# A GNN kernel: one wait, one load and two subtractions in other places of their queues

## The reference

```python
edge_index = jnp.stack([src, dst])
x = _layernorm(x + _L0_gnn_ref(x, src, dst, ...))       # attention, 12 heads of 64 channels
x = _layernorm(x + _L1_gnn_ref(x, edge_index, ...))     # 4 heads of 256, then 1 head of 768
```

```python
e = leaky_relu(a1[src] + a2[dst])
w = exp(e - segment_max(e, dst)[dst])
agg = segment_sum(w[:, :, None] * ft[src], dst) / segment_sum(w, dst)
```

## Time and profile before

| what | value |
|---|---|
| median of 3 runs | 1193.08 us (1192.1 to 1193.24) |
| profiled execution | 1192.1 us |
| its span, first to last instruction | 1190.3 us |
| PE busy | 1085.8 us, 91% |
| DVE busy | 993.9 us, 84% |
| ACT busy | 654.5 us, 55% |
| POOL busy | 145.4 us, 12% |
| mean granted clock of PE | 0.976 |

### The profile page before, as it was taken

One profiled execution on the slowest core, in us unless ns is written; L12 is line 12 of the kernel. 1 busy time (PEld: TensorE's weight loads), 2 busy tenths in 40 slices (PEclk: granted clock), 3 DMA queues, 4 the chain that ended last, 5 costly groups with the idle time before them and its releaser, 6 DMA issues.

```text
span 1190.3 us, 20787 instructions
## 1 busy us (share of the span) xinstructions
PE 1085.8 (91%) x7873; PEld 910.2 (76%) x7873; DVE 993.9 (84%) x1698; ACT 654.5 (55%) x1070; POOL 145.4 (12%) x155
## 2 busy tenths in 40 slices
PE   6887679988898898799999999999989999999996
PEld 3443556666666666699999899999978888788885
DVE  6988999999999999894884799999797765277864
ACT  6444989999899999422200377676712311232431
POOL 1000000000000000000036021020500025321111
PEclk9999879999999999999999999999989999999998
DMA  3011302020202110653045510204052024245111
GB/s 140 27 62 47 130 2 87 1 88 1 87 5 84 38 55 7 219 176 126 28 142 195 208 43 2 80 1 142 2 177 67 28 78 168 78 147 177 67 64 50
DMA packets 39858, 98.94 MB, mean 83 GB/s; under 512 B 4467, under 2 KB 17147, under 8 KB 39765
## 3 DMA queue, kind: packets, MB, share of 16 engines
q1 hardware_dynamic: 39766, 97.66, 24.1%
HBM read 70.74 MB, written 26.90 MB: 82 GB/s over the span
## 4 chain that ended last, share of the span: by engine, by line
PE 59%; DVE 25%; issue 10%; ACT 3%; DVEq 1%; DMA 1%; POOL 0%; SPq 0%; POOLq 0%; ACTq 0%
PE psum L1005 13%; PE psum L922 13%; PE psum L970 12%; DVE R L1539 12%; PE psum L1033 9%; DVE R L1525 6%; PE psum L701 3%; PE psum L955 3%; PE psum L986 1%; ACT R L1154 1%; PE psum L805 1%; PE psum L1016 1%; ACT R L1170 1%; DVE LC L1503 1%; DVE R L1401 1%
## 5 line engine op out<-in xcount | busy, mean ns | idle before, releaser
L864 PE MATMUL psum<-ident,R 128*128 128x128 f32 (+3 forms) x1200 | 161.0, 284 | 45.1 <-ACT R L1154 44.9
L864 PEld LDWEIGHTS psum<-ident,R 128*128 128x128 f32 (+3 forms) x1200 | 130.7, 144 | 86.8 <-ACT R L1154 74.2
L1539 DVE CUSTOM_DVE_ANT_0 R<-R,LC 128x1250 f32<-128x1250 f32 x120 | 176.0, 1468 | 0.0
L1154 ACT ACTIVATE R<-R,row_max 128x1250 f32<-128x1250 f32 x120 | 161.4, 1345 | 5.2 <-DVE row_max L1539 4.0
L878 PE MATMUL psum<-R 128*64 128x256 f32 (+3 forms) x1200 | 149.5, 388 | 0.0
L1170 ACT COPY R<-psum 128x1280 f32<-128x1280 f32 x120 | 143.3, 1194 | 1.5 <-PE psum L864 1.5
L922 PE MATMUL psum<-w_hi,x1T_hi 128*128 128x256 f32 (+1 forms) x480 | 136.3, 284 | 2.7 <-issue 1.6
L922 PE MATMUL psum<-w_lo,x1T_hi 128*128 128x256 f32 (+1 forms) x480 | 135.0, 281 | 0.0
L922 PE MATMUL psum<-w_hi,x1T_lo 128*128 128x256 f32 (+1 forms) x480 | 134.9, 281 | 0.0
L1525 DVE SCALAR_TENSOR_TENSOR R<-R 128x1250 f32<-128x1250 f32 x80 | 122.5, 1532 | 0.0
L1986 POOL TENSOR_TENSOR rstd<-rstd,minus_half 128x1 f32<-128x1 f32 (+1 forms) x40 | 30.5, 763 | 712.2 <-DVE rstd L1552 712.2
(11 more groups left out here) (223 smaller groups left out, 2569.8 us busy)
## 6 DMA issues: line engine op xcount, KB each, us to landing
R<-rows_spill SPq DMA_DIRECT2D x20, 625.0 KB, 5.2
rowbuf<-rows_spill SPq DMA_DIRECT2D x14, 625.0 KB, 5.3
lc_spill<-LC SPq DMA_DIRECT2D x9, 625.0 KB
LC<-lc_spill SPq DMA_DIRECT2D x9, 625.0 KB, 5.8
res_spill<-colbuf SPq DMA_DIRECT2D x36, 128.0 KB, 2.4
R<-res_spill SPq DMA_DIRECT2D x9, 512.0 KB, 3.4
R<-in_x_dram SPq DMA_DIRECT2D x1, 3456.0 KB
res_spill<-R SPq DMA_DIRECT2D x9, 384.0 KB
```

Source lines behind the costliest of these rows:

```text
L864: last = e.transpose(turn0[r % 2][0:m, s, 0:n_dst], ring[0:n_dst, r % RING0, s * P:s * P + m], ident[0:n_dst, 0:n_dst])
L1154: e.activation(ring[0:m, r % RING0, :], ring[0:m, r % RING0, :], ACT.Exp, bias=row_max[0:m, r % RING:r % RING + 1], scale=-1.0, accum_out= ...
L1539: e.tensor_tensor_reduce(slot, slot, LC[0:m, i, :], 1.0, MIN_CEILING, ALU.add, ALU.min, row_max[0:m, r % RING:r % RING + 1]).then_inc(S.le ...
```

## The change

It moves things and takes none out but one wait. In `dve_program` DVE waits for `cleared` to be 3, not 2, ahead of the count, and the waits inside the first addition go. In `sync_program` `load_w1(0)` and its wait go ahead of `store_x1(0)`. In the part that makes x1, `rest_w1(1)` goes ahead of `first_sum(1)`, and `rest_w1(0)` ahead of `first_norm(1)`. In `turn_after1` tile 1 is transposed (on PE, and kept on ACT) after product (2, 0) and no longer after (1, 0).

```diff
-        turn_after1 = {(2, i): i + 1 for i in range(1, NT - 2)}
-        turn_after1[(1, 0)] = 1
+        turn_after1 = {(2, i): i + 1 for i in range(NT - 2)}
         turn_after1[(0, NT - 2)] = NT - 1
...
             load_x0(4)
+            e.wait_ge(S.turned0, ROWS0 - 1)
+            load_w1(0)
             for i in range(NT):
...
                 store_x1(i)
                 if i == 0:
-                    e.wait_ge(S.turned0, ROWS0 - 1)
-                    load_w1(0)
                     for t in range(5, 9):
                         load_x0(t)
...
-            def add(g, half, first=False):
-                if first:
-                    e.wait_ge(S.cleared, 3)
+            def add(g, half):
                 e.wait_ge(S.win_free, g * GT + GT)
...
-                        add(g + (-1), 1 - half, first)
+                        add(g + (-1), 1 - half)
...
-            group(1, 1, True)
+            group(1, 1)
...
-                if g == 0:
-                    e.wait_ge(S.cleared, 3)
...
-            e.wait_ge(S.cleared, 2)
+            e.wait_ge(S.cleared, 3)
             span = e.value_load(base_i[0:1, GROUPS:GROUPS + 1], min_val=0, max_val=N)
...
             rest_x1(0)
+            rest_w1(1)
             for i in range(1, NT):
                 first_sum(i)
-                if i == 1:
-                    rest_w1(1)
                 if 1 < i < 4:
                     rest_x1(i - 1)
                 first_stats(i)
+                if i == 1:
+                    rest_w1(0)
                 if i >= 4:
                     rest_x1(i - 1)
                 first_norm(i)
-                if i == 1:
-                    rest_w1(0)
```

More of the change, by code:

```diff
@@ L1411, in add, with group @@
                 e.tensor_tensor(window_, window_, window_psum(half), ALU.add).then_inc(S.win_added, 1)
-            def group(g, half, first=False):
+            def group(g, half):
                 for j in range(GT):
```

## The result

The change makes the kernel slower. Its median is 1199.1 us (1197.73 to 1202.31, six runs), beside 1193.62 us (1192.1 to 1194.94, six runs) of the kernel before; the ratio over all executions on record, 25 of the kernel after, is 1.0054 with an interval of 1.0039 to 1.0068, that is 6.4 us, 4.7 to 8.1 (the two medians alone lie 5.5 apart). The forecast was slower by 4.4, with a range that ended at 6.2. The profiled execution of the kernel after took 1199.95 us with a span of 1198.1, 7.8 us more than the span before.

What follows compares the result with a forecast made beforehand. DVE was taken to set the pace in the edge count and up to 516.07, before gemm1. Start 2.6 plus second place 1.8 made +4.4 us, 1197.5 by the median, range 1194.6 to 1199.3.

Steps and rivals of the forecast that it cites:

- Step 1: Start of the edge count: DVE's wait for the third clear delays everything behind it, +2.6 us, bounds 1.6 to 3.0.
- Step 2: Before gemm1: w1 block 0's load goes out earlier, gemm1 starts near 489.5 not 492.37; gain on PE, not the chain.
- Step 3: Store of x1 tile 0, behind 768 KB of load, lands +1.3 us later, bounds 0 to 3.0; DVE waits for it.
- Step 4: DVE, rest_w1(1) ahead of first_sum(1): same 1.67 us instruction 3.3 us earlier, input ready; nothing either way.
- Step 5: DVE, rest_w1(0) ahead of first_norm(1): fills GpSimd wait, later work 0.7 us earlier; x1 tile 1 ready later, 497.1 with store.
- Step 6: Tile 1's transposes before the second product: PE waits till 497.1, clock drops; 516.07 moves +1.8, bounds -0.7 to +3.6.
- A: Rival, chance 0.22: start's delay passes, second place even or better; +1.9 to +3.2 us, about 1195.6.
- B: Rival, chance 0.10: start's delay is absorbed before 124 us; +1.8 or less, 1194.9.
- C: Rival, chance 0.05: PE's earlier first product sets the end, second place -2.9; -0.3 in sum, down to 1190.2.
- D: Rival, chance 0.03: nothing measurable, both places under 0.5 us; needs the clearing complete when DVE asks.

Runs made afterwards that it cites:

- e1: Kernel before with one edit: DVE waits for the third clear ahead of the count; ratio 1.0028 to before, +3.3 us.
- e3: Kernel before with load_w1(0) issued ahead of store_x1(0) and nothing else; ratio 1.0033 to before, +3.9 us.
- e10: Kernel before with the load of w1 block 0 issued from ACT's queue, ahead of the store on SP's queue; ratio 1.0011 to before, +1.3 us.
- e11: Kernel before with the load of w1 block 0 halved, 384 KB ahead of the store and 384 behind; ratio 1.0012 to before, +1.4 us.
- e12: Kernel before with load_w1(0) ahead of store_x1(0) and first_sum(1) ahead of rest_x1(0) on DVE; 1193.03 us, ratio 0.9987 to before.
- e4: Kernel before with the new orders of rest_w1 and of tile 1's transposes, load and store as before; ratio 1.0012 to before, +1.4 us.
- e7: Kernel after with the start of before and rest_w1(0) behind first_norm(1) again; ratio 1.0019 to the kernel before, +2.3 us.

## Why the prediction was right in sign and too low

- **Step 1, the start, +2.6**: right in mechanism. 15.03 for 15.0, and e1 alone costs 3.3 (1.5 to 5.2). The size rests on one profile whose first one-hot was the earliest of twelve; against their mean the delay is 2.1. The first leaky0 came at 128.31, not 127.0: 1.26 us that came with PE's lower clock after the count, which no step has.
- **Step 2, the load, issued at 480.5, landed about 486, gemm1 at 489.5**: the issue was right and the landing wrong. It took 7.6 us where I reckoned 5.5, since I moved 768 KB at 375 GB/s and the stretch had 235 to 296, shared with the store and the x0 loads; for the 0.9 us to the landing, too, the prediction shows no row. ACT kept 1.34 us of idle time and PE gained 1.4, not 2.9. As step 2 says, this gain isn't on the chain; e3 shows that, with PE's first product earlier and a longer time.
- **Step 3, "+1.3 us. Bounds: 0 ..., 3.0"**: this is the term that was mis-sized. The mechanism, a store held up by the bytes of a load ahead of it, is shown (e3, e10, e11, e12), and even the 1.1 us between the two landings was about right (0.96). But the store took 6.10 us for 3.18, +2.9, at my upper bound, since the load ahead of it lands 2.1 us later than I took. I had the row for it, the 6.8 us of the earlier trace rows, and used it for the bound only. The rule in step 3's aside, the order within a ring, isn't needed: from the other queue the load costs 2.5 of the 3.0 us.
- **Step 4, nothing**: not contradicted; no run moves rest_w1(1) alone.
- **Step 5, the subtraction fills 0.66 us of idle time, -0.7**: failed. It took the power and the subtraction to run side by side. GpSimd's power takes 2.0 us beside this subtraction, so the norm waits 0.45 us after it. From the table of the stretch: the norm and the subtraction were done 24.11 us after the last leaky0 before, 23.98 in e4. The gain is 0.1.
- **Step 6, PE waits for tile 1 and its clock falls**: right. The idle time was 6.17 us ("4 us or more"), the clock fell to 0.50, and from the transposes to the product it took 525.80 - 505.17 = 20.63 us, for which I had 19.3 + 1.4 = 20.7. Only the hand-over was late: 499.4 net for 497.1, of which 1.6 is step 3's and 0.5 step 5's; 0.2 I haven't traced. That PE's lateness would outweigh DVE's rests on the traces; no run leaves out the new place of the transposes alone.
- **The sum**: 2.65 + 3.98 = 6.6 us by the two places, +6.4 measured. I had 2.6 + 1.8. The 2.2 missing are steps 3 (1.6) and 5 (0.5). That 6.6 meets 6.4 so closely is in part luck: with the mean start it is 6.1, and the single times of e7 and e10 lie 1.7 to 1.8 us under what their traces say. The rest of the profile's 7.8, +3.10 ahead of the last leaky0 and -1.9 at the end, are differences between single executions, which cancel in part.

Of the rivals, A fell with the 6.10 us of the store and B with e1; C fell as argued, the first product being earlier in e3 and the kernel slower; D fell with the first one-hot and the stretch. That PE sets the end and not DVE holds for the kernel after, by 0.8 us (DVE's low part of tile 3 is there at 525.0, the product starts at 525.80); e7 shows that the margin is thin.

Three things stay open: why the store of tile 2 lands after 3.9 to 4.3 us in e4, e7 and e12 and after 2.3 before, since no run isolates what it meets; whether the low clock at 117 to 126 us is likelier with the late start (it is there in both profiles with the late start, and in 4 of the 12 without it, with a fifth in part); and the times of e7 and e10, above.

## What to carry to other kernels

A load issued earlier isn't free because its target buffer is: ask which transfer in flight somebody waits for, and add all the bytes in flight with it, at the rate of that stretch and not the best one. Before an engine's order is changed to fill an idle gap, look for what runs on the neighbour in that gap, and whether the trace has the same pair side by side elsewhere. A wait that can't be shortened is best covered: first_sum(1) in front of it brought back 2.6 of the 3.0 us of the stretch that moving the load had cost. And a term read from one profile, like the start's 2.6, is to be read in a second one first.

## What the runs showed of the hardware

GpSimd's power of 128x1 elements takes 0.55 us while DVE waits for it, and 2.00 beside a DVE subtraction of 1.75 us with both inputs in SBUF; it then ends 0.41 us after the subtraction does. GpSimd's timeline after, first the stretch of x1, then layer 2:

```profile
487.40 0.55 POOL L1980 TENSOR_TENSOR rstd<-rstd,minus_half 128x1 f32<-128x1 f32 x1 [482.15 <-DVE rstd L1547]
502.40 2.00 POOL L1980 TENSOR_TENSOR rstd<-rstd,minus_half 128x1 f32<-128x1 f32 x1 [14.45 <-DVE rstd L1547]
510.74 0.55 POOL L1980 TENSOR_TENSOR rstd<-rstd,minus_half 128x1 f32<-128x1 f32 x1 [6.34 <-DVE rstd L1547]
...
939.01 2.06 POOL L1980 TENSOR_TENSOR rstd<-rstd,minus_half 98x1 f32<-98x1 f32 x1 [9.96 <-DVE rstd L1547]
```

The last line stands beside a subtraction of DVE too (wr_lo<-LC,wr_hi, from 938.85), and the kernel before had the same pair, 2.06 us at 931.13: the price of step 5 was to be read there. Beside another subtraction of DVE, whose first input is in PSUM, the power keeps its 0.55 us. The timeline of the kernel before has both, and so has that after (the power at 524.20):

```profile
515.05 0.96 DVE L1626 TENSOR_TENSOR x1T_lo<-psum,x1T_hi 128x768 fp32r<-128x768 f32 x1
...
515.21 0.55 POOL L1986 TENSOR_TENSOR rstd<-rstd,minus_half 128x1 f32<-128x1 f32 x1 [5.60 <-DVE rstd L1552]
```

DVE doesn't slow down beside the power (1.75 us either way). The Trainium skill ("GPSIMD Engine Reference", "1. Specifications") has GpSimd share its interfaces to SBUF with DVE and names DVE instructions with two SBUF inputs as what it contends with; the trace agrees, 2.00 us with two inputs in SBUF and 0.55 with one. No run moved an input of the same subtraction, and the two differ in size as well, so that the second input is the cause is supported and not isolated.

Transfers in flight together: with the load of 768 KB issued 2.5 us ahead, the store of 384 KB takes 6.1 us, where it took 3.18 ahead of the load, and the load takes 7.6. Issued from two queues (e10) the store still takes 5.7 and the load 6.8. And PE's granted clock over the same transposes, after the count, was 1.00 in some executions and 0.50 in others of kernels that differ by nothing between the first one-hot and there. From the first one-hot to the first leaky0 it was 113.0 to 113.3 us in the six profiles at the lower level and 110.8 to 112.3 in the seven at the full one: a profile's difference in a place that nobody edited is to be checked against a second profile before it is explained.
